# A gather of edge rows on GpSimd: blocks signalled in pairs, with a wait for the landing behind every eighth gather

## What is computed

```python
edge_index = jnp.stack([src, dst])            # src random, dst sorted; dst = 6250 * u**2
x = x + gnn0(layernorm(x), ...)   # sum over the edges of h[src] + relvectors[edge_type], then a GRU cell
x = x + ffn0(layernorm(x), ...)   # shared MLP + 4 experts, top 2
x = x + gnn1(layernorm(x), W, b)  # sum over the edges of (x @ W.T + b)[src], divided by degree + 1
x = x + ffn1(layernorm(x), ...)   # 8 experts, hidden 1024, top 2

# the part that matters here, once in each layer:
red = jax.ops.segment_sum(table[src], dst, num_segments=6250)
```

## Time and profile before

| | us |
|---|---|
| Time, median of 3 runs | 3987.14 (3972.49 to 4001.89) |
| Span of the profiled execution | 4051.2 |
| TensorE matmul busy | 2468.4 (61%) |
| VectorE busy | 1525.7 (38%) |
| ScalarE busy | 778.7 (19%) |
| GpSimd busy | 1836.0 (45%) |
| First graph stage, first gather to last | 142.9 to 1900.8 |
| Second graph stage, first gather to last | 1968.2 to 3238.6 |

### The profile page before, as it was taken

How to read it: one execution, slowest core, us unless ns; L and a number is a source line. 1 busy time by engine, 2 the same in 40 slices (tenths; PEclk the granted TensorE clock), 3 DMA queues, 4 the chain that set the end, 5 groups by cost and what they waited for, 6 DMA issues and landing times. The chain is left out here.

```text
span 4051.2 us, 54160 instructions
## 1 busy us (share of the span) xinstructions
PE 2468.4 (61%) x13318; PEld 1805.0 (45%) x13319; DVE 1525.7 (38%) x3970; ACT 778.7 (19%) x1414; POOL 1836.0 (45%) x2044
## 2 busy tenths in 40 slices
PE   1177776766665556444366555555444369999992
PEld 1055454544343334322234333333222159999992
DVE  6344343333333223221244443333232145555545
ACT  1122222221111112100101000000000034444441
POOL 0343333344334544455455556565666624444441
PEclk7578887777776767666567776766666579999996
DMA  4321111122212221222322223232323322112215
GB/s 131 93 59 58 54 55 44 49 63 60 60 49 62 80 64 58 64 79 70 81 84 83 79 82 91 77 89 86 91 86 88 91 72 64 63 63 63 62 43 204
DMA packets 157828, 303.02 MB, mean 75 GB/s; under 512 B 47365, under 2 KB 91816, under 8 KB 157752
## 3 DMA queue, kind: packets, MB, share of 16 engines
q0 software_dynamic: 85984, 234.74, 19.9%
q1 hardware_dynamic: 40876, 36.11, 2.9%
q10 hardware_dynamic: 30892, 31.40, 2.4%
HBM read 261.73 MB, written 40.39 MB: 75 GB/s over the span
## 5 line engine op out<-in xcount | busy, mean ns | idle before, releaser
L743 POOL DMA_INDIRECT rows<-table,srcT x1568 | 1534.0, 978 | 1504.4 <-PE bank L811 942.0
L811 PE MATMUL bank<-rows,onehot 128*128 x3904 | 791.3, 335 | 734.5 <-issue 597.4
L811 PEld LDWEIGHTS bank<-rows,onehot 128*128 x3904 | 422.2, 108 | 1095.6 <-issue 960.5
L772 DVE SCALAR_TENSOR_TENSOR onehot<-iota_row,tbase,dstT 128x512 f16 x488 | 367.2, 753 | 995.2 <-issue 555.6
L1773 PE MATMUL bank<-xe_high,W_high 128*128 128x256 f32 x864 | 252.5, 292 | 30.4 <-DVE xe_low L1851 30.1
L1774 PE MATMUL bank<-xe_low,W_high 128*128 128x256 f32 x864 | 250.6, 290 | 0.0
L1775 PE MATMUL bank<-xe_high,W_low 128*128 128x256 f32 x864 | 250.2, 290 | 0.0
L1773 PE MATMUL bank<-W_high,hid_high 128*128 128x256 f32 x864 | 248.3, 287 | 0.0
L1823 ACT ACTIVATE hid<-bank,b 128x256 f32<-128x256 f32 x432 | 181.6, 472 | 346.3 <-PE bank L1775 345.6
L1775 PE MATMUL bank<-W_high,hid_low 128*128 128x256 f32 x864 | 243.9, 282 | 0.0
L1774 PE MATMUL bank<-W_low,hid_high 128*128 128x256 f32 x864 | 243.8, 282 | 0.0
(11 more groups left out here) (338 smaller groups left out, 3695.7 us busy)
## 6 DMA issues: line engine op xcount, KB each, us to landing
rows<-table,srcT POOLq DMA_INDIRECT x1568
W<-in_L_ffn_W_dram SPq DMA_DIRECT2D x14, 1024.0 KB
y<-results ACTq DMA_DIRECT2D x12, 1024.0 KB, 9.9
x_res<-in_x_dram SPq DMA_DIRECT2D x1, 6144.0 KB, 43.8
out_dram<-x_res SPq DMA_DIRECT2D x12, 512.0 KB
table<-part ACTq DMA_DIRECT2D x11, 512.0 KB
normal<-xn ACTq DMA_DIRECT2D x11, 512.0 KB
table<-part SPq DMA_DIRECT2D x6, 512.0 KB, 2.9
```

Of the source, the lines that this page charges most:

```text
L743: nc.gpsimd.indirect_dma_start(out=rows[:, k % (M * U), 0:ROW], out_offset=None, in_=q.table, in_offset=bass.IndirectOffsetOnAxis(srcT[:, ...
L772: last = nc.vector.scalar_tensor_tensor(onehot[:, ds(slot, U), :], iota_row[:, :].unsqueeze(1).to_broadcast([P, U, P]), base, dstT[:, ds(k ...
L811: last = nc.tensor.matmul(acc[:, 0:cols], hot, ring_rows[:, ds(row0 + (s * q.pitch + at), cols)], start=False, stop=False, skip_group_chec ...
```

## The change

The diff is whole:

```diff
 def program(nc, a, out):
-    assert NT == GROUPS * GW + 1 and EP * EJ * P >= NE and BLOCKS % LANDED == 0 and M == MH and PASS % M == 0
+    assert NT == GROUPS * GW + 1 and EP * EJ * P >= NE and BLOCKS % LANDED == 0 and BLOCKS % 2 == 0 and M == MH and PASS % M == 0
...
                     pool.wait_ge(q.used, pool.value_load(frees[0:1, i:i + 1], min_val=1, max_val=NT * (PASS + 1) + MH))
                     settled(pool)
                     for s in range(U):
+                        if i % 2 == 1 and s == U // 2:
+                            ready(i - 1, 1)
                         k = i * U + s
                         nc.gpsimd.indirect_dma_start(
                             out=rows[:, k % (M * U), 0:ROW], out_offset=None, in_=q.table,
                             in_offset=bass.IndirectOffsetOnAxis(srcT[:, k:k + 1], axis=0)).then_inc(q.landed[i % LANDED], 16)
-                    if i > 0:
-                        ready(i - 1, 1)
-                ready(BLOCKS - 1, 1 + PASS - BLOCKS)
+                    if i % 2 == 1:
+                        ready(i, 1 if i < BLOCKS - 1 else 1 + PASS - BLOCKS)
```

## The result

The changed kernel took **3775.47 us** (median of four, 3769.0 to 3792.94) against 3979.81 us (3958.06 to 4001.89) of the kernel before on the same chip: ratio 0.9488, interval 0.9445 to 0.953. The forecast was 3892 us, its range ended at 3785. The profiled span is 3767.9 us, against 4051.2. The spans are thus 283 us apart and the medians 204: the profiled execution of the kernel before took 1.8% more than the median of its runs, so differences of stages against the earlier trace rows come out too large, by up to some 80 us for both stages together.

What follows compares the result with a forecast made beforehand. Neither stage was taken as bound by GpSimd; engines lag while gathers stream. Stage gains of -82 and -15 us sum to -97: 4051 to 3954, times 0.984 gives 3892 us, range 3785 to 4030.

Steps and rivals of the forecast that it cites:

- I take 40% of the lag: Both graph stages: share of lag the pauses relieve; -82 us in the first, -15 us taken in the second.
- The lag: Nameless TensorE idle time before gather matmuls, less 0.4 us a visit: 218 us in the first stage, 174 in the second.
- The 20 us of ScalarE: First stage, window 0: ScalarE copies its sum 20 us late while GpSimd gathers without a pause.
- the pause of 2.92 us: Second stage, kernel before: a gather pause said to be enough for TensorE's matmuls to recover.
- the halving: A lag beginning anywhere in a pair of 12.7 us was said to end after 6.3 us on average.
- full relief: Rival, chance 0.17: lags hardly begin any more; first stage -180 us, second -34, giving 3776 us.
- The scaling by 0.984: Turns the forecast span into a median time: 3954 us becomes 3892.
- The pause: Behind every eighth gather: landing 1.8 plus waking 0.85 is 2.65 us in place of 0.30, so 2.35 us more.
- slower: Rival, chance 0.15: pause near 3.7 us extra, GpSimd bounds the second stage, +98 us there; 4093 us.
- Behind the sixth gather: Wait for the fourth gather's landing, covered by two gathers: cost 0, without that cover up to 0.85 us.
- Hidden in the first stage: First stage: gathers with pauses need 1228 us against 1758, so the pauses cost only some 5 us.
- No relief: Rival, chance 0.27: pauses too short, each lag ends when it would have; +5 to +15 us a stage, 4007 us.

Runs made afterwards that it cites:

- e1: Against the kernel before: each block but the last signalled behind the second gather of the next, no landing wait behind the eighth; 4044.95 us, ratio 1.0031.
- e2: Against the kernel before: signals left in their old places, only a wait for the landing added behind every eighth gather; 3799.04 us, ratio 0.9414.
- e12: The kernel before, unchanged, profiled on a chip without lag; 3282.15 us.
- e4: Against the changed kernel: a pause behind each block in place of every second; 4219.1 us, ratio 1.0458 to the kernel before.
- e6: Against the changed kernel: the next slot's wait placed ahead of the landing's wait; 3720.36 us, ratio 0.921 to the kernel before.
- e13: The changed kernel, unaltered, on a chip without lag; 3720.38 us, ratio 1.1314 to the kernel before.
- e17: Against the kernel before: at most five blocks gathered ahead in place of eight; 4072.42 us, ratio 1.0051.

## Why the prediction was wrong

The mechanism was right where there is lag: the pause, and not the signals, relieves it (e1, e2). But an unbroken stream does not make it by itself: in e12 784 gathers follow each other at 0.30 us without lag. **The step that failed is "I take 40% of the lag"**, in what it took for the lag and in the share.

*The lag.* It was put at 218 and 174 us, the nameless idle time before gather matmuls less 0.4 us a visit. Against a chip without lag the stages are 508 and 261 us longer. Four things were missed. A visit without lag has (54.1 + 13.6) / 488 = 0.14 us before it, not 0.4. Lag also stands on other lines: the three rows of the kernel before shown above are 174.7 us together, the three of the changed kernel 35.1. And PE is busy longer, 1086 us in the first stage of the kernel before, 963 in e12's. Two things are mixed in that. Creeping matmuls count as busy: those of L929 on `wihT_high` take 413 ns against 386, and 386 again in e4, which has hardly any lag and as low a clock. And TensorE's granted clock is lower, 0.73 against 0.86 (0.78 after the change, 0.75 in e4): those of L1016 on `sW_high` take 407 ns, 321 in e12 and still 357 in e4. And in the second stage half of the lag hides in what would be waits for GpSimd (above). The 20 us of ScalarE were read in the earlier trace rows and not priced.

*The share.* Of the first stage's 508 us 454 were relieved, 89%; in the second nothing of the 261 is left in the length, where GpSimd's bound covers what remains. The nearest row, the pause of 2.92 us in the earlier trace rows, was the right one; the halving (a lag that begins anywhere in a pair) was wrong, since few lags begin any more (124 pieces of nameless idle time in the first stage, against 308 in the earlier trace rows). That is what the rival *full relief* said. Its time, 3776 us, is the measured one by luck, twice over: it gave -180 and -34 where the stages gave -311 and +30, and its span, 3837 us, is 69 us over the profiled 3767.9. The scaling by 0.984 took 61 us off, while the changed kernel's profiled execution was no slower than its runs.

*The pause.* The 2.15 us from a gather's end to TensorE's start, from which the landing was reckoned, held exactly. The sum with the waking, 2.65 us, held too, once the read of `frees` and the wait on `used` are ahead of it (2.6 us in e6). These two the forecast named as queued behind the wait and priced at nothing; they are 0.6 us. The pause is 2.9 us extra, over the 2.7 from which the *slower* rival decides: GpSimd did become the bound of the second stage (PE waits 517.5 us for its signals; POOL waits only 19.6 us for PE, against 233.0 in the earlier trace rows), and the stage lost 30 us where -15 was forecast. As priced, 1006 + 98 x 2.9 = 1290 against 1301 measured.

*Behind the sixth gather.* Costed at nothing, and right: e1, with such a wait in each block, took 1.0031 (0.9991 to 1.0072).

*"Hidden in the first stage."* Wrong: the pauses cost 143 us there without lag, and with lag PE waits for GpSimd's signals 172.4 us, against 20.1. Some 156 of the 172.4 us lie in the last third of the stage. The sum over the whole stage (1228 against 1758) hid that the later windows need rows faster than the early ones.

*No relief* is refuted here by the nameless idle time, 597 to 165 us. What no row could show is that the kernel before has another time on other chips.

The Trainium skill, DMA: Bandwidth & Descriptors, Rules for kernel authors, has the rule to issue early and wait late. Without lag the runs agree: waiting in pairs costs 13% (e13). Where there is lag they do not: the same pairs gain 5%.

The cause of the lag isn't settled. The Trainium skill, Runtime: NRT & Kernel Launch, Instruction fetch mechanics (a branch to a page that isn't buffered forces a DMA), offers a delayed fetch. The profiles count 57 + 19 packets of instructions with lag and without alike; how long they took they don't show, so no run here tests it. Nor is it known what differs between the chips.

## What to carry to other kernels

Idle time that no instruction explains is a term of its own: price it on all engines, and find its floor in a profile without it before taking a share. Run the kernel before on more than one chip before tuning against such a lag: here the same edit is 5% faster on one chip and 13% slower on another, and no version that was run is best on both (before: 3288 us without lag; four memsets: 0.9123 with it). When a wait is put behind work that was issued ahead, price the whole chain to the next issue, register reads and met waits too, and hoist what does not depend on it. And see that an experiment's edit did what it was made for before reading its time: e17's bursts were as long as before.

## What was not expected of the hardware

- The same kernel takes 3280.95 to 3292.64 us on one chip, 3289.98 us (median) on a second, and 3958 to 4073 on all other chips, nearly all of the difference in the two graph stages; the rest of the profiled executions, from the last gather of the second stage on, is 813 us with lag and 808 without.
- With lag, halving a gather's bytes (1.0049) or its rows (1.0134) gives nothing, while 0.37 us of memsets behind each gather gives 9%.
- A gather of 64 rows takes GpSimd 941 ns, one of 128 rows 978 ns.
- The pages with lag differ in one thing more: none of the 15 gives a landing time for the loads of `W`, and all five without lag do (7.4 to 8.1 us). Whether the two have one cause is open.
